# Another order of the attention steps in a chain of 16 transformer-like layers on one core

## What is computed

```
x = x + L0_attn_a(ln(x));  x = x + L0_ffn(ln(x));  x = x + L0_attn_b(ln(x));  x = x + L0_ffn(ln(x))
x = x + L1_attn_a(ln(x));  x = x + L1_ffn(ln(x));  x = x + L1_attn_b(ln(x));  x = x + L1_ffn(ln(x))
x = x + L2_attn_a(ln(x));  x = x + L2_ffn(ln(x));  x = x + L2_attn_b(ln(x));  x = x + L2_ffn(ln(x))
x = x + L3_attn_a(ln(x));  x = x + L3_ffn(ln(x));  x = x + L3_attn_b(ln(x));  x = x + L3_ffn(ln(x))
```

```
scores = jnp.einsum('bqhd,bkhd->bhqk', q, k)
scores = jnp.where(mask, -jnp.inf, scores)          # in L3_ffn only
attn = jax.nn.softmax(scores / np.sqrt(HEAD_DIM), axis=-1)
ctx = jnp.einsum('bhqk,bkhd->bqhd', attn, v).reshape(b, t, EMB)
return ctx @ wo + bo
```

## Time and profile before

| | us |
|---|---|
| Median of 3 runs | 4714.01 |
| Lowest and highest | 4685.55, 4722.16 |
| The profiled execution | 4722.16 |
| Its span on the core | 4720.3 |
| PE busy in it | 4199.7 (89%) |
| DVE busy | 3025.4 (64%) |
| ACT busy | 2421.4 (51%) |
| POOL busy | 1125.9 (24%) |

### The profile page before, as it was taken

How to read it: one execution, slowest core, us unless ns; L and a number is a source line. 1 busy time by engine, 2 the same in 40 slices (tenths; PEclk the granted TensorE clock), 3 DMA queues, 4 the chain that set the end, 5 groups by cost and what they waited for, 6 DMA issues and landing times.

```text
span 4720.3 us, 62755 instructions
## 1 busy us (share of the span) xinstructions
PE 4199.7 (89%) x23278; PEld 2020.2 (43%) x23280; DVE 3025.4 (64%) x6690; ACT 2421.4 (51%) x4189; POOL 1125.9 (24%) x1579
## 2 busy tenths in 40 slices
PE   8899879999899989999886778998989989789999
PEld 5222346555522246555542235555543334333343
DVE  4899457677489957775347975666666652466622
ACT  3588634455358854554445543554535553246632
POOL 1100123333200023332124641111130004420034
PEclk8799988899789988998888998999988889879889
DMA  1100102111110021110000000000010000010000
GB/s 50 28 18 12 46 35 47 32 33 35 38 24 22 8 64 36 34 38 12 11 5 0 0 8 8 16 9 16 19 35 22 22 1 0 29 28 22 9 1 9
DMA packets 48018, 104.09 MB, mean 22 GB/s; under 512 B 15064, under 2 KB 15064, under 8 KB 46432
## 3 DMA queue, kind: packets, MB, share of 16 engines
q1 hardware_dynamic: 46560, 98.49, 7.6%
q10 hardware_dynamic: 1152, 1.57, 0.2%
HBM read 40.24 MB, written 1.05 MB: 9 GB/s over the span
## 4 chain that ended last, share of the span: by engine, by line
PE 58%; DVE 23%; ACT 12%; POOL 3%; issue 2%; DMA 1%; ACTq 1%; SPq 0%; POOLq 0%; DVEq 0%
PE PS L450 29%; DVE SM L1200 6%; PE PS L1126 6%; PE PS L1074 5%; ACT AR L1174 3%; ACT AR L457 3%; PE PS L1106 3%; PE PS L2647 3%; DVE AR L2451 2%; DVE AR L454 2%; PE PS L1760 1%; PE PS L1750 1%; PE PS L477 1%; PE PS L1804 1%; PE PS L1109 1%
## 5 line engine op out<-in xcount | busy, mean ns | idle before, releaser
L1200 DVE TENSOR_REDUCE SM<-PS 128x1 f32<-128x512 f32 (+3 forms) x1792 | 1027.1, 627 | 247.7 <-PE PS L1079 133.9
L450 PE MATMUL PS<-AR,WS 128*128 128x512 f32 (+1 forms) x2112 | 1058.8, 640 | 80.2 <-DVE AR L454 30.9
L1174 ACT ACTIVATE AR<-PS 128x1024 f32<-128x1024 f32 (+3 forms) x896 | 796.7, 931 | 320.0 <-PE PS L1106 203.4
L457 ACT ACTIVATE AR<-PS 128x512 f32<-128x512 f32 (+4 forms) x728 | 439.6, 614 | 524.6 <-PE PS L450 401.6
L450 PEld LDWEIGHTS PS<-AR,WS 128*128 128x128 f32 (+1 forms) x2112 | 401.7, 202 | 542.0 <-issue 410.6
L1074 PE MATMUL PS<-AR 51*128 51x512 bf16 (+3 forms) x1792 | 496.3, 394 | 82.2 <-DVE SM L1200 36.8
L1126 PE MATMUL PS<-AR 128*32 128x512 f32 (+3 forms) x3584 | 458.2, 585 | 1.0 <-ACT AR L1174 1.0
L1831 ACT ACTIVATE AR<-PS,SM 128x128 f32<-128x128 f32 x512 | 229.6, 452 | 440.8 <-DVE SM L1894 433.4
L1074 PEld LDWEIGHTS PS<-AR 51*128 51x128 bf16 x1792 | 125.6, 94 | 605.6 <-DVE SM L1200 408.3
L1106 PE MATMUL PS<-AR 51*128 51x512 bf16 (+3 forms) x1792 | 315.8, 377 | 17.8 <-ACT AR L1174 8.7
L1233 POOL CAST MBT<-SM 128x8 bf16<-128x8 f32 x128 | 28.1, 220 | 1228.9 <-DVE SM L1204 614.7
(11 more groups left out here) (323 smaller groups left out, 7170.9 us busy)
## 6 DMA issues: line engine op xcount, KB each, us to landing
TP<-RAW SPq DMA_DIRECT2D x512, 64.0 KB, 2.0
AR<-AR SPq DMA_DIRECT2D x720, 32.0 KB
WS<-wall SPq DMA_DIRECT2D x4, 3654.5 KB, 11.2
WS<-wall SPq DMA_DIRECT2D x8, 902.5 KB, 4.5
WS<-wall SPq DMA_DIRECT2D x2, 3334.5 KB, 11.1
WS<-wall SPq DMA_DIRECT2D x1, 2384.0 KB, 8.7
WS<-wall SPq DMA_DIRECT2D x1, 1543.5 KB, 6.2
AR<-AR ACTq DMA_DIRECT2D x48, 32.0 KB
```

The costliest lines, as they stand in the source:

```text
L450: t = e.matmul(o, l, r, start=(n == 0), stop=(n == len(pairs) - 1))
L457: return e.activation(o, i, ACT.Copy, scale=1.0)
L1174: e.activation(pv[:, :, off:512], sv[:, :, off:512], ACT.Exp, scale=scale).then_inc(*F.at_exp.up((s, u, p2)))
L1200: e.tensor_reduce(mh[:, at, k0 // 512:k0 // 512 + 1], bank(ring(n + g), m), AX.X, ALU.max, negate=True).then_inc(*F.at_max.up((s, k, i, rr ...
```

## The change

The diff, cut:

```
-STEPS = ("max", "front0", "front1", "max", "back")
...
-    cost = lambda p: (min(512, 128 * (p[1] + 1) - p[3]) if causal else 512) + 90
-    lead, behind = (8, 5) if causal else (20, 3)
...
-        while kti == 0 and not {("rows", k, 4 * qc + 1), ("rows", k, 4 * qc + 3)} <= {(x[0],) + x[2:] for x in out}:
...
-        for kind in STEPS:
...
+                waiting.append((now + 4, "rows", 1, k, i))
...
+                if (k, qc) == (3, 1):
+                    for c in range(2):
+                        waiting.append((h + 6 + 4 * c, "turn", 1, c))
+                        waiting.append((h + 9 + 4 * c, "out", 1, c))
...
+    put("finish", 1, 7, 1)
+    for c in (2, 3):
+        put("turn", 1, c)
+    for c in (2, 3):
+        put("out", 1, c)
```

More of the change, by code:

```diff
@@ L321, in attention_order @@
              for k0 in range(0, 128 * (i + 1) if causal else 1024, 512)]
-    cost = lambda p: (min(512, 128 * (p[1] + 1) - p[3]) if causal else 512) + 90
-    width = lambda u: 512 - max(0, 128 * u[2] - 512 * u[1]) if causal else 512
-    lead, behind = (8, 5) if causal else (20, 3)
-    out, due, taken, clock = [], [], [0], [0]
+    wide = lambda p: (min(512, 128 * (p[1] + 1) - p[3]) if causal else 512) + 90
+    halves = 2 * len(units)
+    rate = sum(wide(p) for p in pairs) / halves
+    begin = {}
+    for n, (k, qc, kti, nk) in enumerate(units):
+        begin.setdefault((k, qc), 2 * n)
+    lead, total = 0, 0
+    for p in pairs:
+        total += wide(p)
+        lead = max(lead, total - rate * (begin[p[0], p[1] // 4] - 7))
+    out, waiting, taken = [], [], [0]
     def put(kind, banks, *args):
@@ L380, in attention_order, with settle, maxima @@
-    put("back", 0, len(units) - 1)
[L381 to L384, removed]
+    def settle(now):
+        for item in sorted([x for x in waiting if x[0] <= now], key=lambda x: x[0]):
+            waiting.remove(item)
+            put(*item[1:])
+    issued, n = 0, 0
+    def maxima(until, now):
+        nonlocal issued, n
+        while n < len(pairs) and issued + wide(pairs[n]) / 2 <= until:
+            k, i, rr, k0 = pairs[n]
+            put("max", 2, *pairs[n])
+            issued += wide(pairs[n])
+            n += 1
+            if i % 2 and rr and (n == len(pairs) or pairs[n][0:3] != (k, i, rr)):
+                waiting.append((now + 4, "rows", 1, k, i))
+            if now < 0:
+                now += 1
+                settle(now)
@@ new lines, in attention_order @@
+    maxima(lead, -1000)
+    rest = [x[0] for x in waiting]
+    for z, x in enumerate(list(waiting)):
+        waiting[z] = (x[0] - max(rest) + 4,) + x[1:]
+    for h in range(halves):
[3 more added lines that the diff above has]
+        if p2 and u:
+            put("back", 0, u - 1)
+            k, qc, kti, nk = units[u - 1]
+            if kti == nk - 1:
+                waiting.append((h + 2, "finish", 1, k, qc))
[4 more added lines that the diff above has]
+        settle(h)
@@ L385, in attention_order @@
+    put("back", 0, len(units) - 1)
+    settle(halves + 100)
+    put("finish", 1, 7, 1)
[3 more added lines that the diff above has]
+        put("out", 1, c)
     return out
```

## The result

The changed kernel takes 4731.97 us in the median of 14 runs, the kernel before 4696.05 in the median of its 14 by then; the ratio is 1.007 with a 95% interval of 1.0055 to 1.0086, so some 33 us slower, by less than 1%. One of the 14 executions took 7250.44 us; it is left out of the ratio, no trace of it exists, and its cause is open. The profiled execution has a span of 4737.0 us, 16.7 more than the one before.

A forecast was written before the change was run, and what follows sets the result against it. Plain stages were taken as bound by VectorE and a TensorE-VectorE loop, both 2.49 us a unit; causal ones fill neither engine. Plain +58, causal -38, ends +2 make +22 on 4714: 4736, own range 4713 to 4761, overall 4660 to 4788.

The forecast's parts named there:

- Plain stages: The two non-causal attention stages: each 29 us longer, about 408 us instead of 379, together +58.
- The loop: Plain unit, TensorE and VectorE sharing three banks: second front between last maximum and back, 2.71 us instead of 2.49.
- The lead: Pairs ahead of the first front: three more per plain stage, +3.9 us; 24 instead of 12 per causal stage, 31 us.
- The stretch without maxima: End of a plain stage: grows from 10.5 to 12 units at 2.0 us, +3 us.
- Causal stages: The two causal attention stages: 37.2 us a head instead of 39.5, 319.5 a stage instead of 339, together -38.
- 3 for the clock to come up: Causal stage after its leading pairs: 3 us allowed for the clock to rise, then full once fronts run.
- Ends: All four stages, third chunk's turn and out moved to the end: +0.5 us each, +2 in all.
- The sum: All four attention stages: plain +58, causal -38, ends +2, giving +22 us and a forecast time of 4736.
- Rival 1: Plain stages: the front hides in the last maximum's own time; -22 us in all, 4692; chance 0.12.
- Rival 2: Causal stages: TensorE's steps alone set the head, 31.1 us, 43 less per stage; 4650; chance 0.11.
- Rival 3: Causal stages: nothing gained, waits for ScalarE's copies after rows steps eat 17 us per stage; 4770; chance 0.17.
- Rival 4: Plain stages: the clock falls as TensorE waits in each unit, 25 us more per stage; 4786; chance 0.08.

The follow-up runs named there:

- the first experiment: New order in the two plain stages only, old order in the causal ones, against the kernel before: ratio 1.0114, +53 us.
- the second experiment: New order in the two causal stages only, old order in the plain ones, against the kernel before: ratio 0.9953, -22 us.
- the two halves: New order in the plain stages only, ratio 1.0114, and in the causal stages only, 0.9953, each against the kernel before.
- its two variants: Changed kernel with both plain-stage fronts ahead of the second pair, ratio 0.9966 to before, or behind it, 4782.23 us beside 4703.71.

## Why the prediction was right, step by step

**Plain stages: right.** The loop of 0.42 + 0.75 + 0.215 + 0.32 + 1.00 = 2.71 is 2.70 in the trace, the unit with one front fewer and one more in it follow the same sum, and eight units take 23.58 against a predicted 23.72; the 4.16 of the unit with finish and rows is 4.06. Two terms beside the loop were too large. The lead cost +1.4 us, not +3.9: I priced three pairs and overlooked that the old lead idled. At each of its two rows steps VectorE had waited 1.25 us; with the rows steps later in the list it does not wait at all (before, then after):

```profile
155.48 8.61 DVE L1200 TENSOR_REDUCE SM<-PS 128x1 f32<-128x512 f32 x14 [1.25 <-PE PS L1074]
```

```profile
146.99 10.03 DVE L1197 TENSOR_REDUCE SM<-PS 128x1 f32<-128x512 f32 x16
```

The stretch without maxima cost +1.8, not +3: by the two lists it grows from 12 units to 13, by one and not by one and a half. Between the two, from the first front to the last pair, the stage grew by 21.2 us (345.2 against 324.0), where I had 22.8. In all +24 and +26 in the profile and +27 by the first experiment, against +29.

**Causal stages: the mechanism right, the size too large.** A head of 37.2 us was forecast; where the clock stays up it takes 37.1. The lead, 31 us, took 29.9. What failed is the step "3 for the clock to come up" and the words "the clock full once fronts run". The clock came up 12 us after the first front in one causal stage and 26 in the other, and then fell again. In the first causal stage three of the seven heads from finish to finish take 41.0 us, at 2.4 GHz for most and at 1.2 for 10 us of it, and one more is hit in part (40.4 against 37.9 us); together some 14 us. In the second stage two heads are hit, together 6 us, and the low clock at the start lasts 55 us, against 41 in the first, for which the first 512 queries take 4.6 us more. Without these losses both stages would take 320 us from the first pair to the last reciprocal (334.4 less 14, 331.2 less 6.3 and 4.6; an estimate), which is the forecast 319.5. So the lengths of the steps and loops were right and the clock was the term that was wrong. By the profile -3 and -7 us came, and by the ratio of the second experiment about -11 per stage (its own profile shows -7), in place of -19. That the old order has such falls too, one in each head (granted 0.91 over a head), I took for a mark of its crowded boundary alone. The new order has a smooth boundary and still falls.

**Ends: nothing.** From the start of the last back to the end of the last transpose of a plain stage 3.3 us lie before and after; I had +0.5.

**The sum.** +22 was forecast, +33 measured: by the ratios of the two halves (+53.5 and -22, together +31.5, within the interval of the whole) the plain stages cost 4 us less than I said, the causal ones gave 16 less and the ends cost 2 less. The errors partly cancel, so the sum is nearer to the result than the causal part is. That the forecast time, 4736, lies 4 us from the measured 4732 is luck: the two medians differ by 36 us and not by 22, and the kernel before has a median of 4696 over 14 executions, where the three that the forecast started from had 4714. The profiled pair shows only +16.7: the four stages are 41 us longer in it, and the rest of the program took 24 us less in that execution, see below.

**The rivals.** Rival 1, that the front hides, is refuted: the same steps with none, one and two fronts in the loop take 2.49, 2.70 and 2.92 us. Rival 2, 31.1 us per head, was not reached even with fronts paired (34.6). Rival 3, nothing gained in the causal stages, was half true, though not through ScalarE's copies, since a head at the full clock took 37.1 us against the 37.2 forecast, these copies included, but through the clock. Rival 4 placed the clock's fall in the plain stages. In none of the eight profiled plain stages of the new order and its two variants did it come once the clock had risen, not even with a wait of 0.57 us in each unit, where both fronts stand behind the second pair. (With the rows steps of both kinds of stage moved it fell once, for 3.4 us, in a plain stage where no maxima were left.) The rule of the Trainium skill that I named with it ("TensorE: Matmul & The Clock Gate", "A second HAM failure mode: psum-queue depth-cycling") thus did not show in the plain ring, and what the causal stages show is of the kind that it describes, a clock that swings while TensorE works through banks with short waits; the measurement decides, and it differs between two stages that use the same ring.

## What to carry to other kernels

When two engines pass a small ring of buffers back and forth, write the loop out: from the first matmul to its reader, to the buffer's release, to the last matmul that needs it, to whatever stands between that and the start of the next round. Work that stands between the late matmul and the end of the round lengthens the round by all of its time; the same work between the two groups of matmuls was free here, where VectorE was full at 2.48 of 2.49 us. Even spacing of steps is no aim in itself: here the evenly spread list lost to one that puts both fronts where TensorE would have waited anyway, and in the causal stages the even pace of pairs and the paired fronts together gave the best kernel, 0.9834.

## What I had not expected

- The same list of steps falls to 1.2 GHz in some heads and not in others. In the new order a fall of 6.8 us made a head 39.5 us instead of 37.1, and one of 6.8 followed by one of 3.4 made it 41.0. Pairing the fronts left no such fall in six stages, beside the 2.5 us per head that it saved by the loop (37.1 to 34.6).
- The sections between the first two attention stages take 754 us in one execution and 737 in another, with the same instructions. Before, then after:

```profile
536.00:1290.00 754.00, 682.45 (x4456) 410.36 (x4455) 487.41 (x1232) 347.84 (x890) 228.00 (x280) 0.86 0.14 39
```

```profile
555.00:1292.00 737.00, 658.89 (x4462) 394.88 (x4461) 488.28 (x1234) 348.40 (x890) 228.91 (x280) 0.90 0.14 40
```

  VectorE, ScalarE and GpSimd are busy for the same time in both; TensorE is not, and its granted clock is 0.86 in one, 0.90 in the other. Of the profiles taken here some lie at one length and some at the other, whichever order the attention stages have. Why the clock differs there is open. That is 17 us, half of the change's whole effect, and the reason why one profile against one profile misjudges it: the ratio over many runs and the lengths of the stages do not.
- Matmuls added to the lead behind those of the pairs, with as many columns each, left the clock at 1.2 GHz for all of its 34 us (granted 0.51). They also made the lead 4 us longer.
